# One TensorE signal per slot in the two gather stages of a two-layer GNN kernel

## The chip, the cores and the metric

The kernel runs on one core of a Trainium2 chip. The metric is the device time of one execution in microseconds (us). A core has five engines, each with its own instruction stream: TensorE (PE in the views, PEld for its weight loads), VectorE (DVE), ScalarE (ACT), GpSimd (POOL) and SyncE (SP, which here only issues DMAs). They meet through semaphores: an instruction or a DMA raises one when it is done, and another engine's stream waits until it has reached a number.

## The reference

Two message passing layers over the same 400,000 edges (sorted by destination) and 12,500 nodes, 64 features, all in float32:

```python
def gnn_layer_0(x, edge_attr, ...):
    msg = mlp(concat([x[row], edge_attr]))          # matmul, batch norm over all edges, SiLU
    agg = segment_sum(msg, col) / max(count(col), 1)
    return mlp(concat([x, agg]))

def gnn_layer_1(x, edge_attr, ...):
    msg = relu(x[src] + edge_attr)
    agg = segment_sum(msg, dst)
    return relu(((1 + eps) * x + agg) @ W.T + b)

x = layernorm(x + gnn_layer_0(x, edge_attr, ...))
x = layernorm(x + gnn_layer_1(x, edge_attr, ...))
```

## The kernel before, in words

The edges are worked off in G = 625 **slots** of EG = 640 edges, TG = 5 tiles of P = 128. There are four large steps, one after the other: **stage A** (L250 to L570) gathers x[src] for every edge, applies the first linear layer and stores the result; pass B (L598 to L720) normalises it, applies SiLU and sums it by segment; a node part (L900 to L1150) makes the new x and writes it to DRAM; **stage C** (L1150 to L1255) gathers the new x for every edge, adds, applies ReLU and sums by segment. A short output part ends the program. The change touches stages A and C alone.

**Stage A, one slot s.** SP loads the slot's edge features into half of the ring buffer `Z` (L357; RING = 10 slots). POOL gathers the 640 rows of x into the other half by five indirect DMAs (L371). PE transposes the five tiles of `Z` into PSUM (`turn_rows`, L399 to L407). ACT copies these five tiles to `ZT` in SBUF (L456; two buffers). PE applies W1 to `ZT` and, by five more small matmuls, counts the edges per destination (`dense`, L409 to L424). DVE takes statistics of two slots at a time, adds the counts into a table and copies the result to `h_ring` (`pair`, L518 to L531), and ACT issues the store of it (L449). DVE also builds the one-hot matrix `hot` that the counts are made with (`one_hot`, L504).

**Stage C, one slot s.** SP loads edge features into `E` (L1174), POOL gathers rows of the new x into `X` by five indirect DMAs (L1194), both rings of 10 slots. PE adds the two in PSUM by two matmuls with the identity (`edge_sum`, L1200 to L1209), ACT applies ReLU (L1235), PE sums by segment with five matmuls (`segment_sum`, L1211 to L1218), DVE adds the result into the table (`add`, L1249) and builds the one-hot matrices (L1244).

**What sets the order.** Every engine's order is written out by hand. On PE it is, in both stages, one step ahead: `turn_rows(s+1)`, `dense(s)`, `turn_rows(s+2)`, `dense(s+1)` and so on (`edge_sum` and `segment_sum` in stage C):

```python
for s in range(slots):
    if not (slots < BODY and s == slots - 1):
        turn_rows(k, s + 1)
    dense(k, s, slots < BODY and s == slots - 1)
```

PE raises **two semaphores per slot**. In stage A `rows_done` rises at the end of `turn_rows` and `dense_done` at the end of `dense`; in stage C `sum_put` rises at the end of `edge_sum` and `summed` at the end of `segment_sum`. Who waits for them:

- SP (L356, L1173) and POOL (L366, L1187) wait for `rows_done` or `sum_put` of the slot ten before, since that frees a place in the ring. POOL's wait is followed by a count of its own (`carry_wait`, L131).
- ACT, before it copies slot s, waits for `rows_done` of slot s and `dense_done` of slot s-2, which frees a buffer of `ZT` (L454, L455). In stage C it waits for `sum_put` of slot s and `summed` of slot s-5.
- DVE waits for `dense_done` (L505, L520) and `summed` (L1243, L1248).
- PE itself waits for the gathered rows, the edge features, ACT's and DVE's signals.

Of the kernel before, what the change touches and what calls it, by code (L numbers as in the profile page):

```python
# [55 lines left out]
def gnn_kernel(nc, x, src, dst, edge, W1, b1, g1, be1, W2, b2, g2, be2, W3, b3, eps1, out):  # L56
# [50 lines left out]
    with ctx:  # L107
# [118 lines left out]
        with ExitStack() as here:  # L226
# [109 lines left out]
            gathered = gathered_x  # L336
            rows_done = sem("rows_done")
            zt_taken = sem("zt_taken")
            dense_done = sem("dense_done")
            h_ready = sem("h_ready")  # L340
# [10 lines left out]
            with nc.Block() as block:  # L351
                @block.sync
                def _(sp):
                    def body(k, slots):
                        for s in range(slots):
                            wait_at(sp, rows_done, k, BODY, s + 1 - RING)  # L356
                            sp.dma_start(Z[:, s % RING, :, D:2 * D], edge_v[at(k, BODY, s)]).then_inc(e_loaded[s % RING], 16)  # L357

                    all_bodies(sp, body)
                    sp.wait_ge(s_x, 16)  # L360

                @block.gpsimd
                def _(pool):
                    for g in range(G):
                        r = g % RING
                        if g >= RING:  # L366
                            pool.wait_ge(rows_done, g + 1 - RING)
                            carry_wait(pool)
# [8 lines left out]
                def _(pe):  # L377
# [21 lines left out]
                    def turn_rows(k, s):  # L399
# [4 lines left out]
                        for j in range(TG):  # L404
                            last = nc.tensor.transpose(banks(2 * (s % 2), 2, P, EG)[:, j * P:(j + 1) * P],  # L405
                                                       Z[:, r, j, :], ident[:, :])
                        last.then_inc(rows_done, 1)  # L407

                    def dense(k, s, alone):  # L409
# [12 lines left out]
                        for j in range(TG):  # L422
                            last = nc.tensor.matmul(PS[0:D, bank + ab, HC:HC + WIN], ones_bf[:, :],  # L423
                                                    hot[:, q % 5, ab, j, :], start=(j == 0), stop=(j == TG - 1))  # L424
                        last.then_inc(dense_done, 1)

# [5 lines left out]

                    turn_rows(0, 0)
                    all_bodies(pe, body)
# [11 lines left out]
                def _(act):  # L446
# [5 lines left out]
                    def body(k, slots):  # L452
                        for s in range(slots):
                            act.wait_ge(rows_done, at(k, BODY, s + 1))  # L454
                            wait_at(act, dense_done, k, BODY, s - 1)  # L455
                            act.activation(ZT[:, s % 2, :], banks(2 * (s % 2), 2, P, EG), ACT.Copy).then_inc(zt_taken, 1)  # L456
                            if s % 2 == 1 and not (isinstance(k, int) and k == 0 and s == 1):
                                store(k, s // 2 - 1)
# [11 lines left out]
                def _(dve):  # L470
# [35 lines left out]
                    def one_hot(k, s):  # L506
                        wait_at(dve, dense_done, k, BODY, s + 1 - 10)
                        nc.vector.tensor_tensor(
# [9 lines left out]
                    def pair(k, q, firsts):  # L518
                        bank = 4 + 2 * (q % 2)
                        dve.wait_ge(dense_done, at(k, BODY, 2 * q + 2))  # L520
                        for c in range(2):
# [9 lines left out]
                    def body(k, slots):  # L531
# [8 lines left out]
                        if slots < BODY:  # L540
                            q = slots // 2
                            bank = 4 + 2 * (q % 2)
                            dve.wait_ge(dense_done, G)
                            nc.vector.bn_stats(stats[:, 6 * (G - 1):6 * G], PS[:, bank, 0:HC]).then_inc(stats_done, 1)
# [609 lines left out]
        with ExitStack() as here:  # L1154
# [6 lines left out]
            gathered = gathered_x1  # L1161
            sum_put = sem("sum_put")
            hot_ready = sem("c_hot_ready")
            msg_ready = sem("c_msg_ready")
            summed = sem("c_summed")
            added = sem("c_added")
            x1_kept = sem("x1_kept")

            with nc.Block() as block:
                @block.sync  # L1170
                def _(sp):
                    def load(k, s):
                        wait_at(sp, sum_put, k, BODY, s + 1 - RING)  # L1173
                        sp.dma_start(E[:, s % RING, :, :], edge_v[at(k, BODY, s)]).then_inc(e_loaded[s % RING], 16)  # L1174
# [11 lines left out]
                def _(pool):  # L1186
                    for g in range(G):  # L1187
                        r = g % RING
                        if g >= RING:
                            pool.wait_ge(sum_put, g + 1 - RING)  # L1190
                            carry_wait(pool)
# [8 lines left out]
                def _(pe):  # L1200
                    def edge_sum(k, s):
# [5 lines left out]
                        pe.wait_ge(gathered[r], at(k, 32 * TG, 16 * TG * (s // RING) + 16 * TG))  # L1207
                        nc.tensor.matmul(PS[:, s % 2, 0:HC], ident[:, :], X[:, r, :, :].rearrange("p t c -> p (t c)"),  # L1208
                                         start=False, stop=True).then_inc(sum_put, 1)  # L1209

                    def segment_sum(k, s):  # L1211
# [3 lines left out]
                        for j in range(TG):  # L1215
                            last = nc.tensor.matmul(PS[D:P, 2 + s % S, 0:WIN], msg[:, s % S, j, :], hot[:, s % S, j, :],  # L1216
                                                    start=(j == 0), stop=(j == TG - 1))
                        last.then_inc(summed, 1)  # L1218

# [5 lines left out]

                    edge_sum(0, 0)
                    all_bodies(pe, body)

                @block.scalar
                def _(act):  # L1230
                    def body(k, slots):
                        for s in range(slots):
                            act.wait_ge(sum_put, at(k, BODY, s + 1))
                            wait_at(act, summed, k, BODY, s + 1 - S)
                            act.activation(msg[:, s % S, :, :].rearrange("p t c -> p (t c)"), PS[:, s % 2, 0:HC],  # L1235
                                           ACT.Relu).then_inc(msg_ready, 1)
# [4 lines left out]
                def _(dve):  # L1241
                    def one_hot(k, s):
                        wait_at(dve, summed, k, BODY, s + 1 - S)  # L1243
                        nc.vector.tensor_tensor(  # L1244
# [4 lines left out]
                    def add(k, s, first):  # L1249
                        dve.wait_ge(summed, at(k, BODY, s + 1))  # L1250
                        wait_at(dve, added, k, BODY, s)
# [205 lines left out]
```

## Time and profile before

| what | value |
|---|---|
| time, median of 3 runs | 10121.98 us (10119.3 to 10125.19) |
| span of the profiled execution | 10108.7 us, 90454 instructions |
| what lies around the span, as against the median | 13.3 us |
| POOL busy | 5970.4 us (59%) |
| PE busy | 4398.6 us (44%) |
| DVE busy | 1864.3 us (18%) |
| ACT busy | 1239.0 us (12%) |
| DMA | 638.49 MB, mean 63 GB/s |

The profile is one execution recorded by the hardware profiler. Its page gives busy time by engine and the costliest groups of instructions; a further view lists who waited for whom, another lists instructions in order of time. The program has one core, so no other core's work stands in the trace. The profiled execution's own time is its span of 10108.7 us plus what lies around it (start and end of the program); the median of the runs is 13.3 us above the span. Releasers are inferred from semaphore events. Where the page cannot place the semaphore it says "remote", or it names a DMA that had used the same semaphore number earlier in the program. A semaphore's true source is read in the code.

### The profile page before, as it was taken

Reading aid. Unit: us, or ns where it says so; the run is one execution under the profiler, and the core shown is the slowest. Engines: PE = TensorE matmul, PEld = TensorE weight load, DVE = VectorE, ACT = ScalarE, POOL = GpSimd, SP = SyncE. Lnnn points to the kernel's source line nnn. Section 1 sums busy time; section 2 is a strip of 40 time slices with the busy share of each in tenths; the row PEclk is TensorE's granted clock in tenths of the full one; section 3 lists DMA queues with packets and bytes.
Section 4 is the critical chain, followed back from the end, with each engine's and each line's share of the span. In section 5 each row is a group of like instructions: output and inputs, shape, how many; then the busy total and the mean of one; then the engine's idle time right before and its main releaser. Section 6 shows DMA issues by size and latency. Waiting matters only on the chain. (4 is left out here: it accounts for less than half of the span.)

```text
span 10108.7 us, 90454 instructions
## 1 busy us (share of the span) xinstructions
PE 4398.6 (44%) x25778; PEld 2780.5 (28%) x25778; DVE 1864.3 (18%) x4868; ACT 1239.0 (12%) x2056; POOL 5970.4 (59%) x6272
## 2 busy tenths in 40 slices
PE   3433443434444444347984333333333334333335
PEld 1222222222222222226872222222222222222222
DVE  2111111111111111116763000000000000000002
ACT  0000000000000000004664000000000000000001
POOL 6666666666666666660003666666666666666662
PEclk7666666666666666668996666666666666666666
DMA  3222222222222222224551121121112212111111
GB/s 79 68 67 66 69 67 66 69 67 67 68 67 68 68 67 67 68 67 132 164 151 50 44 47 45 45 45 45 45 45 45 45 45 46 44 45 45 45 45 33
DMA packets 800217, 638.49 MB, mean 63 GB/s; under 512 B 532451, under 2 KB 618703, under 8 KB 799368
## 3 DMA queue, kind: packets, MB, share of 16 engines
q1 hardware_dynamic: 553308, 326.50, 12.0%
q0 software_dynamic: 200416, 208.55, 10.7%
q10 hardware_dynamic: 46400, 102.52, 3.1%
q14 instruction: 75, 0.61, 0.0%
q8 instruction: 18, 0.29, 0.0%
HBM read 528.15 MB, written 108.90 MB: 63 GB/s over the span
## 5 line engine op out<-in xcount | busy, mean ns | idle before, releaser
L1194 POOL DMA_INDIRECT X<-x_scratch,src_idx x3125 | 2971.8, 951 | 1624.3 <-issue 893.6
L371 POOL DMA_INDIRECT Z<-in_x_dram,src_idx x3125 | 2968.4, 950 | 1611.1 <-issue 895.1
L416 PE MATMUL PS<-ZT,W_sb 128*64 128x320 f32 x2500 | 1198.0, 620 | 2716.5 <-ACT ZT L456 2391.7
L1216 PE MATMUL PS<-hot_c,msg_c 128*64 128x48 f32 x6250 | 658.9, 271 | 2765.6 <-issue 1733.5
L1216 PEld LDWEIGHTS PS<-hot_c,msg_c 128*64 128x64 f32 x6250 | 575.0, 184 | 3163.0 <-issue 2048.4
L416 PEld LDWEIGHTS PS<-ZT,W_sb 128*64 128x64 f32 x2500 | 396.7, 185 | 3153.5 <-issue 2160.2
L522 DVE BATCH_NORM_STATS2 stats<-PS 128x320 f32 (+1 forms) x624 | 279.3, 490 | 3670.2 <-remote 3451.3
L456 ACT ACTIVATE ZT<-PS 128x640 f32<-128x640 f32 x625 | 425.2, 702 | 4150.2 <-remote 3395.5
L1252 DVE TENSOR_TENSOR table<-table,PS 64x48 f32 x625 | 130.2, 208 | 4057.3 <-DMA shares_scratch<-counts 3495.7
L1235 ACT ACTIVATE msg_c<-PS 128x320 f32<-128x320 f32 x625 | 260.0, 436 | 4295.3 <-DMA counts_scratch<-table 2919.9
L1205 PE MATMUL PS<-E,ident 128*128 128x320 f32 x1250 | 689.6, 644 | 11.8 <-DMA E<-in_edge_attr_dram 11.8
L405 PE MATMUL PS<-ident,Z 128*128 128x128 f32 x3125 | 635.1, 350 | 6.9 <-issue 6.9
L1208 PE MATMUL PS<-X,ident 128*128 128x320 f32 x1250 | 586.9, 560 | 24.4 <-DMA X<-x_scratch,src_idx 18.6
L405 PEld LDWEIGHTS PS<-ident,Z 128*128 128x128 f32 x3125 | 447.6, 178 | 254.5 <-issue 226.3
L650 PE MATMUL PS<-hot,msg 128*64 128x48 f32 x6250 | 427.2, 224 | 0.0
L650 PEld LDWEIGHTS PS<-hot,msg 128*64 128x64 f32 x6250 | 388.3, 138 | 52.6 <-issue 36.6
L977 POOL DMA_DIRECT2D counts_scratch<-table x1 | 0.6, 583 | 675.4 <-POOLq L123 675.4
L1208 PEld LDWEIGHTS PS<-X,ident 128*128 128x128 f32 x1250 | 320.5, 257 | 192.8 <-issue 118.8
L616 ACT ACTIVATE mT<-hT,shift_col,scale_col 128x640 f32<-128x640 f32 x313 | 285.2, 911 | 3.7 <-DMA hT<-h_scratch 3.7
L1244 DVE TENSOR_TENSOR hot_c<-window,rel 128x240 f32<-128x240 f32 x625 | 256.1, 410 | 114.9 <-issue 89.6
L527 DVE TENSOR_SCALAR h_ring<-PS,b1c 128x640 f32<-128x640 f32 x312 | 271.8, 871 | 0.0
L423 PEld LDWEIGHTS PS<-hot_a,ones_bf 128*64 128x64 bf16 x3125 | 226.5, 139 | 151.6 <-issue 128.1
(135 smaller groups left out, 2519.8 us busy)
## 6 DMA issues: line engine op xcount, KB each, us to landing
Z<-in_edge_attr_dram SPq DMA_DIRECT2D x625, 160.0 KB
E<-in_edge_attr_dram SPq DMA_DIRECT2D x625, 160.0 KB
h_scratch<-h_ring ACTq DMA_DIRECT2D x312, 320.0 KB
hT<-h_scratch SPq DMA_DIRECT2D x312, 320.0 KB
Z<-in_x_dram,src_idx POOLq DMA_INDIRECT x3125
X<-x_scratch,src_idx POOLq DMA_INDIRECT x3125
x_nodes<-in_x_dram SPq DMA_DIRECT2D x1, 3125.0 KB
x_ring<-in_x_dram SPq DMA_DIRECT2D x25, 125.0 KB
```

Of the source, the lines that this page charges most:

```text
L371: nc.gpsimd.indirect_dma_start(out=Z[:, r, j, 0:D], out_offset=None, in_=x, in_offset=bass.IndirectOffsetOnAxis(ap=src_idx[:, n:n + 1], ax ...
L405: last = nc.tensor.transpose(banks(2 * (s % 2), 2, P, EG)[:, j * P:(j + 1) * P], Z[:, r, j, :], ident[:, :])
L416: nc.tensor.matmul(PS[ab * D:(ab + 1) * D, bank + c, 0:HC], W1_sb[:, :], ZT[:, s % 2, c * HC:(c + 1) * HC], start=True, stop=True)
L456: act.activation(ZT[:, s % 2, :], banks(2 * (s % 2), 2, P, EG), ACT.Copy).then_inc(zt_taken, 1)
L522: nc.vector.bn_stats(stats[:, ds(at(k, 120, 12 * q + 6 * c), 6)], PS[:, bank + c, 0:HC]).then_inc(stats_done, 1)
L527: nc.vector.tensor_scalar(h_ring[:, q % 5, :].rearrange("p (c e) -> p c e", c=2), PS[:, bank:bank + 2, 0:HC], b1c[:, :], None, ALU.add).th ...
L616: act.activation(mT[0:parts, q % 5, :], hT[0:parts, q % 5, :], ACT.Silu, bias=shift_col[0:parts, :], scale=scale_col[0:parts, :]).then_inc ...
L650: last = nc.tensor.matmul(PS[D:P, 4 + 2 * (q % 2) + ab, 0:WIN], msg[:, q % 5, j, ab, :], hot[:, q % 5, ab, j, :], start=(j == 0), stop=(j ...
L1194: nc.gpsimd.indirect_dma_start(out=X[:, r, j, :], out_offset=None, in_=x1_dram, in_offset=bass.IndirectOffsetOnAxis(ap=src_idx[:, n:n + 1] ...
L1205: nc.tensor.matmul(PS[:, s % 2, 0:HC], ident[:, :], E[:, r, :, :].rearrange("p t c -> p (t c)"), start=True, stop=False)
L1208: nc.tensor.matmul(PS[:, s % 2, 0:HC], ident[:, :], X[:, r, :, :].rearrange("p t c -> p (t c)"), start=False, stop=True).then_inc(sum_put, 1)
L1216: last = nc.tensor.matmul(PS[D:P, 2 + s % S, 0:WIN], msg[:, s % S, j, :], hot[:, s % S, j, :], start=(j == 0), stop=(j == TG - 1))
```

## The change

In both stages PE raises one semaphore per slot, `pe_step`, in place of two. It rises once after the first slot's transposes (`turn_rows(0, 0)`, or `edge_sum(0, 0)`), and then at the end of each `dense(s)` or `segment_sum(s)`. So the value s + 1 now says that `dense(s-1)` is done, and, since PE works in the order above, that `turn_rows(s)` is done too. All waits are moved to it. POOL and SP now wait for the `dense` that follows the transposes of the slot ten before. ACT waits for `dense(s-1)` before it copies slot s, where it waited for `turn_rows(s)` and `dense(s-2)`. No matmul, copy or DMA is added, removed or moved in any engine's order; wait instructions and the register arithmetic for their numbers change.

```diff
@@ stage A @@
-            rows_done = sem("rows_done")
+            pe_step = sem("a_pe_step")
             zt_taken = sem("zt_taken")
-            dense_done = sem("dense_done")
...
-                            wait_at(sp, rows_done, k, BODY, s + 1 - RING)
+                            wait_at(sp, pe_step, k, BODY, s + 1 - RING)
...
-                            pool.wait_ge(rows_done, g + 1 - RING)
+                            pool.wait_ge(pe_step, g + 1 - RING)
...
                             last = nc.tensor.transpose(banks(2 * (s % 2), 2, P, EG)[:, j * P:(j + 1) * P],
                                                        Z[:, r, j, :], ident[:, :])
-                        last.then_inc(rows_done, 1)
+                        return last
...
                             last = nc.tensor.matmul(PS[0:D, bank + ab, HC:HC + WIN], ones_bf[:, :],
                                                     hot[:, q % 5, ab, j, :], start=(j == 0), stop=(j == TG - 1))
-                        last.then_inc(dense_done, 1)
+                        last.then_inc(pe_step, 1)
...
-                    turn_rows(0, 0)
+                    turn_rows(0, 0).then_inc(pe_step, 1)
...
-                            act.wait_ge(rows_done, at(k, BODY, s + 1))
-                            wait_at(act, dense_done, k, BODY, s - 1)
+                            act.wait_ge(pe_step, at(k, BODY, s + 1))
...
-                        wait_at(dve, dense_done, k, BODY, s + 1 - 10)
+                        wait_at(dve, pe_step, k, BODY, s + 2 - 10)
...
-                        dve.wait_ge(dense_done, at(k, BODY, 2 * q + 2))
+                        dve.wait_ge(pe_step, at(k, BODY, 2 * q + 3))
...
-                            dve.wait_ge(dense_done, G)
+                            dve.wait_ge(pe_step, G + 1)
@@ stage C @@
-            sum_put = sem("sum_put")
+            pe_step = sem("c_pe_step")
...
-            summed = sem("c_summed")
...
-                        wait_at(sp, sum_put, k, BODY, s + 1 - RING)
+                        wait_at(sp, pe_step, k, BODY, s + 1 - RING)
...
-                            pool.wait_ge(sum_put, g + 1 - RING)
+                            pool.wait_ge(pe_step, g + 1 - RING)
...
-                        nc.tensor.matmul(PS[:, s % 2, 0:HC], ident[:, :], X[:, r, :, :].rearrange("p t c -> p (t c)"),
-                                         start=False, stop=True).then_inc(sum_put, 1)
+                        return nc.tensor.matmul(PS[:, s % 2, 0:HC], ident[:, :],
+                                                X[:, r, :, :].rearrange("p t c -> p (t c)"), start=False, stop=True)
...
-                        last.then_inc(summed, 1)
+                        last.then_inc(pe_step, 1)
...
-                    edge_sum(0, 0)
+                    edge_sum(0, 0).then_inc(pe_step, 1)
...
-                            act.wait_ge(sum_put, at(k, BODY, s + 1))
-                            wait_at(act, summed, k, BODY, s + 1 - S)
+                            act.wait_ge(pe_step, at(k, BODY, s + 1))
...
-                        wait_at(dve, summed, k, BODY, s + 1 - S)
+                        wait_at(dve, pe_step, k, BODY, s + 2 - S)
...
-                        dve.wait_ge(summed, at(k, BODY, s + 1))
+                        dve.wait_ge(pe_step, at(k, BODY, s + 2))
```

## Rows read from the trace of the kernel before

**Rows 1.** The page: span and busy time of each engine.
```profile
span 10108.7 us, 90454 instructions
PE 4398.6 (44%) x25778; PEld 2780.5 (28%) x25778; DVE 1864.3 (18%) x4868; ACT 1239.0 (12%) x2056; POOL 5970.4 (59%) x6272
```

**Rows 2.** The page's groups: line, engine, operation, count | busy, mean ns | idle before, releaser.
```profile
L1194 POOL DMA_INDIRECT X<-x_scratch,src_idx x3125 | 2971.8, 951 | 1624.3 <-issue 893.6
L371 POOL DMA_INDIRECT Z<-in_x_dram,src_idx x3125 | 2968.4, 950 | 1611.1 <-issue 895.1
```

**Rows 3.** The waits: engine, line <- releaser: us in total, times, longest us.
```profile
POOL Z L371 <- issue: 895.1, 2938, 0.3
POOL Z L371 <- remote: 694.6, 180, 9.9
POOL X L1194 <- DMA counts_scratch<-table: 643.7, 168, 11.6
...
ACT msg L622 <- PE PS L644: 216.9, 312, 1.3
```

**Rows 4.** Timeline of POOL: start us, us, line, operation [idle before <-releaser].
```profile
2004.07 0.94 POOL L371 DMA_INDIRECT Z<-in_x_dram,src_idx  x1 [0.30 <-issue]
2009.63 1.11 POOL L371 DMA_INDIRECT Z<-in_x_dram,src_idx  x1 [4.62 <-remote]
...
2033.59 0.98 POOL L371 DMA_INDIRECT Z<-in_x_dram,src_idx  x1 [0.30 <-issue]
2039.01 0.95 POOL L371 DMA_INDIRECT Z<-in_x_dram,src_idx  x1 [4.44 <-remote]
```

**Rows 5.** Timeline of PE and ACT about the first of these two stops.
```profile
1987.84 0.77 PE L405 MATMUL PS<-ident,Z 128*128 128x128 f32 x5
1995.33 2.39 PE L416 MATMUL PS<-ZT,W_sb 128*64 128x320 f32 x4 [6.72 <-issue]
1997.91 1.33 PE L405 MATMUL PS<-ident,Z 128*128 128x128 f32 x5
...
1994.50 0.70 ACT L456 ACTIVATE ZT<-PS 128x640 f32<-128x640 f32 x1 [10.02 <-remote]
2008.86 0.70 ACT L456 ACTIVATE ZT<-PS 128x640 f32<-128x640 f32 x1 [13.65 <-remote]
```

**Rows 6.** Timeline of pass B, where POOL has no work: PE, then ACT.
```profile
4701.31 0.77 PE L644 MATMUL PS<-ident,mT 128*128 128x128 f32 x5
4702.19 0.49 ACT L622 ACTIVATE msg<-PS 128x384 f32<-128x384 f32 x1 [0.69 <-PE PS L644]
```

**Rows 7.** Timeline of ACT between the two stops, and of PE behind one copy.
```profile
2010.29 0.70 ACT L456 ACTIVATE ZT<-PS 128x640 f32<-128x640 f32 x1 [0.74 <-DVE h_ring L527]
2013.14 0.70 ACT L456 ACTIVATE ZT<-PS 128x640 f32<-128x640 f32 x1 [2.14 <-issue]
2019.87 0.70 ACT L456 ACTIVATE ZT<-PS 128x640 f32<-128x640 f32 x1 [6.03 <-remote]
2038.24 0.70 ACT L456 ACTIVATE ZT<-PS 128x640 f32<-128x640 f32 x1 [17.66 <-remote]
...
92.05 0.70 ACT L456 ACTIVATE ZT<-PS 128x640 f32<-128x640 f32 x1 [29.50 <-remote]
...
94.99 0.46 PE L423 MATMUL PS<-hot_a,ones_bf 128*64 128x48 bf16 x5
```

**Rows 8.** Timeline of the start of stage C: ACT, DVE, PE.
```profile
5471.37 0.44 ACT L1235 ACTIVATE msg_c<-PS 128x320 f32<-128x320 f32 x1 [10.28 <-PE PS L1208]
5487.27 0.44 ACT L1235 ACTIVATE msg_c<-PS 128x320 f32<-128x320 f32 x1 [15.47 <-DMA counts_scratch<-table]
5526.47 0.44 ACT L1235 ACTIVATE msg_c<-PS 128x320 f32<-128x320 f32 x1 [38.76 <-DMA counts_scratch<-table]
...
5476.83 0.21 DVE L1252 TENSOR_TENSOR table<-table,PS 64x48 f32 x1 [30.58 <-DMA shares_scratch<-counts]
5515.39 0.21 DVE L1252 TENSOR_TENSOR table<-table,PS 64x48 f32 x1 [37.91 <-DMA shares_scratch<-counts]
...
5469.90 1.43 PE L1208 MATMUL PS<-X,ident 128*128 128x320 f32 x2 [8.21 <-DMA X<-x_scratch,src_idx]
5471.26 1.30 PE L1216 MATMUL PS<-hot_c,msg_c 128*64 128x48 f32 x10
5479.73 1.43 PE L1208 MATMUL PS<-X,ident 128*128 128x320 f32 x2 [5.80 <-issue]
```

## The prediction, on record before the changed kernel was run

> **What bounds the kernel now.** I read the page first. POOL is busy 59% of the span, more than any other engine, and PE 44% [rows 1]. The page's two largest groups are POOL's gathers of stages A and C, 3,125 each, with 2968.4 + 1611.1 us and 2971.8 + 1624.3 us of busy and idle time [rows 2]. So stage A takes 4579.5 us of POOL's stream and stage C 4596.1 us, together 9175.6 of 10108.7 us. All else (pass B, nodes, output) is 933 us and not touched.
>
> Then the waits tell of what the idle time is made. A gather costs 0.95 us plus 0.30 us of issue (895.1 us in 2938 times), so 1.25 us, and a slot of five 6.25 us. This part is POOL's own. The other part is waits for a place in the ring, which PE's signal frees: 694.6 us in 180 times in stage A, 643.7 us in 168 times in stage C [rows 3]. (The releaser is called "remote" and "DMA counts_scratch"; by the code it is `rows_done` and `sum_put`.)
>
> The timeline of POOL shows their rhythm: a stop of 4.62 us, 20 gathers without a pause, a stop of 4.44 us [rows 4]. From 2009.63 to 2039.01 are 29.38 us for four slots, or 7.35 us a slot; 4579.5 / 625 is 7.33. So the kernel is bound by POOL, plus one stop of some 4.4 us every four slots.
>
> Why does POOL stop? Not because PE is slow: it is idle more than half the time. PE's **signals come late**. At 1994.50 ACT copies a slot, PE works on the copy at 1995.33 and transposes the slot after the next at 1997.91. The transposes of the next slot had therefore been those that ended at 1987.84 + 0.77 = 1988.61. ACT's copy of that slot starts at 2008.86, 20.2 us later, after 13.65 us of idle time [rows 5]. Its second condition, the `dense` before the last, was older still. In pass B, where POOL does nothing, the transposes end at 4702.08 and ACT starts at 4702.19, 0.11 us later, and no such wait exceeded 1.3 us in 312 [rows 3, 6]. So while POOL gathers, a signal of PE can take ten to twenty us, and when POOL has stopped the pending ones arrive together.
>
> The lateness grows with the number of signals in line. At the start of stage C both signals can be read from their readers. The first `edge_sum` in these rows ends at 5471.33 and ACT starts at 5471.37. The `segment_sum` behind it ends at 5472.56; DVE starts at 5476.83, 4.3 us late. The next `edge_sum` ends at 5481.16; ACT starts at 5487.27, 6.1 us late. Then signals wait behind each other, and the readers start at 5515.39 and 5526.47 [rows 8]: 28 and 11 us between deliveries, and (5526.47 - 5471.37) / 4 = 13.8 us a signal over the four. In the steady cycle it is mixed: ACT's four copies start at 2010.29, 2013.14, 2019.87 and 2038.24 [rows 7]. The first few signals after a stop pass quickly, later ones only one in 14 us or so, or with the next stop.
>
> **The change, part by part.** It takes away 625 signals in each stage, 1,250 in all, adds none, and moves no instruction. ACT has one wait less a slot, which is under its 13 to 30 us idle stretches [rows 5, 7] and costs or gives nothing. Three effects are left.
>
> *Fewer signals in line.* A cycle of four slots needs eight signals now. By my reading three to four come with the stop (the rows of ACT at 2008.86 and 2010.29 are of such a group) and four to five while POOL works 25 us. With one signal a slot, the same four to five deliveries beside POOL's work free four to five slots, not two.
>
> *A chain of signals.* ACT's copy of slot s now waits for `dense(s-1)`, and `dense(s)` waits for that copy. So at most one signal is pending at a stop, and the stop frees one slot, not two. A slot costs at least the way from ACT's start to the end of `dense`: 95.45 - 92.05 = 3.40 us [rows 7]. That lies under POOL's 6.25 us. In stage C the same way is 0.44 us and 1.30 us of matmul [rows 8], shorter.
>
> *A later release of the ring place*, by one `dense` (about 3 us of those 3.40). POOL stands there only when it is at a stop, and there the chain above counts it already: nothing more.
>
> The sum: a cycle after the change has 1 slot from the stop and 4 to 5 from deliveries beside POOL, so N = 5 to 6. With the same stop of 4.4 us, a slot costs (6.25 N + 4.4) / N = 7.13 us for 5 and 6.98 us for 6. I take the middle, 7.05, against 7.35: 0.30 x 1,250 = 375 us less. 10108.7 - 375 = 9733.7 of span, plus the 13.3 us around it by which the median of the runs exceeds it: **9747 us**. The bounds of the unknown price, N = 4 and N = 8 (the nearest rows give 4 now, and 8 is one stop in a ring's length), give 7.35 and 6.80 us: 10122 and 9434 us.
>
> What a signal costs PE itself is not on the path, since PE idles. The trace shows delays of 4 to 20 us, and pending signals arriving within one stop [rows 5, 8]. The Trainium skill (TensorE: Matmul & The Clock Gate, Part 3, "The cost: per-tile semaphore tail") fits about 26 ns for every increment on a matmul; by it 1,250 fewer would be 33 us of an engine with slack, and the sum would be no change. The measured delays speak against that being the whole price here.
>
> **The rivals.**
>
> *The stops vanish (chance 0.23).* If signals 6.25 us apart always pass as the one at 5471.33 did (nothing had been signalled for 10 us), POOL never waits. Then the two sums of waits go, less the 0.30 us of issue that each of the 348 would still have: 694.6 + 643.7 - 104.4 = 1234 us, so 8888 us. For it: the quick deliveries after a pause. Against it: the 6.1 us delay of the signal at 5481.16 came with none in line before it, 4.3 us after the last delivery, and 3.40 + 6.1 is more than 6.25.
>
> *The chain is too slow (0.15), slower than before.* If what holds signals back is how long POOL has been working and not how many were sent, then the first 8 us after a stop let pass what PE can make in that time, and that is now a chain of 3.40 us and more a slot: two slots; with the one that the stop frees, three. Then N = 3 and a slot costs (18.75 + 4.4) / 3 = 7.72 us: +0.37 x 1,250 = +460, or 10584 us. It decides where the third link's signal is held until the stop. For it: before the change PE had up to four signals in line to make use of a stop, now one. Against it: 2019.87 is 10 us after POOL's restart and a signal still came through [rows 4, 7].
>
> *The count does not matter (0.12).* Both effects cancel or signals are cheap, as the skill's rule has it. What the stop frees falls from two slots to one, what passes beside POOL rises from two to three, N stays 4: 10122 us.
>
> *The forecast (0.50)*: its own range is 9434 to 10122 us.
>
> **How the numbers follow.** 0.2% of the time, 20 us, is about what can be told from no change. The forecast gives 0.46 faster and 0.02 each to same and slower; the vanished stops 0.23 faster; the slow chain 0.15 slower; the cancelling 0.03 faster, 0.06 same, 0.03 slower. Sum: faster 0.72, same 0.08, slower 0.20. The range starts at 8850, just below the case without stops, and ends at 10400, which leaves out the slow chain's full price and holds the rest.
>
> **What would show it.** In the profile after: the stops of POOL fewer than 348 (about 230 for N = 5.5), each still near 4.4 us; runs of 25 to 30 gathers between them; POOL's busy time and 0.30 us of issue unchanged; ACT's copies still late by many us, but for `dense`. The rival without stops would show POOL's waits for the ring near zero. The slow chain would show runs of 15 gathers. I am wrong in kind if the runs of gathers stay 20 long, or if POOL's stops grow in length rather than number.

## The result, and the profile after

| | before | changed | ratio |
|---|---|---|---|
| time, median (4 runs each, same chip) | 10121.97 us | 10178.03 us (10173.78 to 10183.75) | 1.0054 [1.0043, 1.0066] |
| span of the profiled execution | 10108.7 us | 10175.0 us | |

The change makes the kernel slower by 0.5%. The forecast was 375 us faster. The page and the two largest groups of its section 5, as in [rows 1, 2]:

```profile
span 10175.0 us, 90051 instructions
PE 4538.9 (45%) x25778; PEld 2854.5 (28%) x25778; DVE 1865.3 (18%) x4868; ACT 1270.3 (12%) x2056; POOL 5995.9 (59%) x6272
...
L1191 POOL DMA_INDIRECT X<-x_scratch,src_idx x3125 | 2973.6, 952 | 1657.4 <-issue 904.7
L370 POOL DMA_INDIRECT Z<-in_x_dram,src_idx x3125 | 2992.0, 957 | 1616.0 <-issue 848.8
```

POOL's stream (busy and idle) grew in stage A from 4579.5 to 4608.0 us and in stage C from 4596.1 to 4631.0 us. These 63.4 us are nearly all of the span's 66.3. The time is lost where it was to be won, in POOL's gathers. The waits of the changed kernel (columns as in [rows 3]):

```profile
POOL Z L370 <- issue: 848.8, 2749, 4.3
POOL Z L370 <- remote: 746.8, 372, 5.9
...
POOL X L1191 <- DMA counts_scratch<-table: 676.6, 167, 10.8
```

The waits for the ring were to go from 348 to about 230. They went up to 539. In stage A they doubled in number and halved in mean length, with 746.8 in place of 694.6 us. But this view also counts gaps of 0.3 us, which is POOL's own issue, where a signal came in just then. Stops of over 1 us are the better count: behind the first 101 gathers, 208 in place of 156 in stage A and 156 in place of 139 in stage C. Now the timeline of POOL in the changed kernel, at the place of [rows 4]:

```profile
2019.77 0.94 POOL L370 DMA_INDIRECT Z<-in_x_dram,src_idx  x1 [4.26 <-remote]
...
2039.11 0.95 POOL L370 DMA_INDIRECT Z<-in_x_dram,src_idx  x1 [0.68 <-issue]
...
2049.12 0.95 POOL L370 DMA_INDIRECT Z<-in_x_dram,src_idx  x1 [4.07 <-remote]
```

From stop to stop are 29.35 us and 20 gathers; before it was 29.38 us and 20 gathers [rows 4]. Half the signals, and here the rhythm is the same. Over the whole stage it is not: before the change 145 of the 155 intervals from stop to stop are of 20 gathers, after it 78 of 207 are of 20, 78 of 15 and 47 of 5. Stage C never had the rhythm of [rows 4], which is of stage A. There the usual run was 25 gathers before the change (97 of 138 intervals) and is 20 after it (148 of 155), as two stops of each show, before and then after:

```profile
8052.23 0.95 POOL L1194 DMA_INDIRECT X<-x_scratch,src_idx  x1 [5.06 <-DMA counts_scratch<-table]
...
8088.45 0.95 POOL L1194 DMA_INDIRECT X<-x_scratch,src_idx  x1 [5.20 <-DMA counts_scratch<-table]
```
```profile
8016.60 0.95 POOL L1191 DMA_INDIRECT X<-x_scratch,src_idx  x1 [4.40 <-DMA counts_scratch<-table]
...
8045.78 0.95 POOL L1191 DMA_INDIRECT X<-x_scratch,src_idx  x1 [4.42 <-DMA counts_scratch<-table]
```

25 gathers in 36.22 us became 20 in 29.18 us: the runs became shorter in both stages, and the pace hardly changed. Last, ACT and PE in the same stretch:

```profile
2018.99 0.70 ACT L454 ACTIVATE ZT<-PS 128x640 f32<-128x640 f32 x1 [9.94 <-remote]
2022.22 0.70 ACT L454 ACTIVATE ZT<-PS 128x640 f32<-128x640 f32 x1 [2.52 <-remote]
2026.97 0.70 ACT L454 ACTIVATE ZT<-PS 128x640 f32<-128x640 f32 x1 [4.04 <-PE PS L422]
2038.33 0.70 ACT L454 ACTIVATE ZT<-PS 128x640 f32<-128x640 f32 x1 [10.66 <-remote]
2048.35 0.70 ACT L454 ACTIVATE ZT<-PS 128x640 f32<-128x640 f32 x1 [9.31 <-remote]
```
```profile
2019.76 0.46 PE L422 MATMUL PS<-hot_a,ones_bf 128*64 128x48 bf16 x5
2027.74 0.34 PE L422 MATMUL PS<-hot_a,ones_bf 128*64 128x48 bf16 x5
```

PE's `dense` ends at 2019.76 + 0.46 = 2020.22 and at 2028.08. ACT's next copies, which wait for just these signals, start at 2022.22 and at 2038.33. By the chain only one signal is ever on its way, and it still needs 2.0 and 10.3 us. So these two are not late because they stand in line behind another.

### The profile page after: what moved, and what is told of

It reads as the page before. It is cut to its first block and busy times, and to the rows that moved or that the text cites. A ratio compares the mean times of both kernels' runs of the same rounds, so it can differ in the third digit from the quotient of the medians.

```text
span 10175.0 us, 90051 instructions
## 1 busy us (share of the span) xinstructions
PE 4538.9 (45%) x25778; PEld 2854.5 (28%) x25778; DVE 1865.3 (18%) x4868; ACT 1270.3 (12%) x2056; POOL 5995.9 (59%) x6272
## 5 line engine op out<-in xcount | busy, mean ns | idle before, releaser
L415 PE MATMUL PS<-ZT,W_sb 128*64 128x320 f32 x2500 | 1224.9, 632 | 2705.7 <-ACT ZT L454 1614.6
L1213 PE MATMUL PS<-hot_c,msg_c 128*64 128x48 f32 x6250 | 688.7, 278 | 2705.5 <-issue 2334.0
L1213 PEld LDWEIGHTS PS<-hot_c,msg_c 128*64 128x64 f32 x6250 | 604.7, 192 | 3123.6 <-issue 2733.2
L1202 PE MATMUL PS<-E,ident 128*128 128x320 f32 x1250 | 724.5, 674 | 11.8 <-DMA E<-in_edge_attr_dram 11.8
L1205 PE MATMUL PS<-X,ident 128*128 128x320 f32 x1250 | 617.6, 587 | 24.6 <-DMA X<-x_scratch,src_idx 17.9
L1202 PEld LDWEIGHTS PS<-E,ident 128*128 128x128 f32 x1250 | 261.5, 261 | 60.3 <-DMA E<-in_edge_attr_dram 12.2
```

The costliest lines, as they stand in the source:

```text
L415: nc.tensor.matmul(PS[ab * D:(ab + 1) * D, bank + c, 0:HC], W1_sb[:, :], ZT[:, s % 2, c * HC:(c + 1) * HC], start=True, stop=True)
L1202: nc.tensor.matmul(PS[:, s % 2, 0:HC], ident[:, :], E[:, r, :, :].rearrange("p t c -> p (t c)"), start=True, stop=False)
L1205: return nc.tensor.matmul(PS[:, s % 2, 0:HC], ident[:, :], X[:, r, :, :].rearrange("p t c -> p (t c)"), start=False, stop=True)
```

## The experiments

All results first. Ratios are against the kernel before on the same chip (its median was 10061.6 to 10062.7 us beside e1 to e6, e10 and e11, and 10119.5 us beside the others, so times of different rows don't compare). Where no ratio stands, one run was made, and the kernel's result is not the reference's, since it leaves out gathered rows.

| run | what it is | time, us | ratio |
|---|---|---|---|
| e1 | the change in stage A alone | 10080.72 | 1.0017 [1.0008, 1.0026] |
| e2 | the change in stage C alone | 10070.92 | 1.0008 [0.9999, 1.0017] |
| e3 | four signals per slot | 10064.14 | 1.0003 [0.9993, 1.0012] |
| e4 | one signal per slot, given early | 10051.94 | 0.9992 [0.9983, 1.0001] |
| e5 | stage C on plain loads, no gather | 6801.45 | |
| e6 | e5, POOL busy with memsets | 7148.75 | |
| e7 | stage C: the sum on VectorE | 10134.59 | 1.0012 [1.0002, 1.0022] |
| e8 | stage A: two slots per round trip | 10110.34 | 0.9991 [0.9981, 1.0000] |
| e9 | e7 and e8 | 10124.47 | 1.0005 [0.9995, 1.0015] |
| e10 | the change again, another chip | 10090.08 | 1.0030 [1.0019, 1.0042] |
| e11 | the chain alone, two signals | 10095.86 | 1.0037 [1.0023, 1.0050] |
| e12 | stage C: gathers that nobody waits for | 10969.02 | |
| e13 | a pause of 0.22 us behind each gather | 10790.18 | 1.0660 [1.0629, 1.0691] |
| e14 | a pause of 0.11 us | 10117.15 | 0.9995 [0.9984, 1.0007] |
| e15 | stage C: each gather half as many rows | 10130.15 | |

### The number of signals, and the chain

**e1** and **e2** are the parts of the change's diff under "stage A" and "stage C", each alone.

> Stage A has one signal per slot, stage C keeps two. The profile of the changed kernel gives stage A 28.5 us more of POOL's stream (4608.0 against 4579.5) and stage C 34.9 us more (4631.0 against 4596.1). If the loss arises in both, each from its own stage: about +29 us, 10151. Rival: only the total counts (what one stage loses shifts the other): anything else, such as no loss here and all of it in stage C.

> Stage C has one signal per slot, stage A keeps two. By its own stage: about +35 us, 10157. Rival as for the run with stage A alone.

Stage A costs 0.17%, some 19 us where 29 were expected; stage C costs 0.08%, some 9 us where 35 were expected, and that can't be told from nothing. The two profiles, taken on one chip, each hold one stage with the change and one without it: POOL's stream is 4563.5 us in stage A with it and 4549.4 without, in stage C 4586.3 and 4572.3. That is 14 us for each stage. Neither part alone carries the loss.

**e10** is the changed kernel again, on the same chip as e11 below (10061.74 us before):

> The changed kernel again, beside the kernel before on the same chip. Its first comparison gave +0.54%; the two stages alone gave +0.17% and +0.08% on another chip. If the parts add, +0.25% here; if the first comparison holds for every chip, +0.5%.

It loses 0.30% there, and 0.54% in the first pair. The sign holds. 0.30% is close to the sum of the parts; why the first pair shows nearly twice as much is open.

**e3** doubles the count: a semaphore that nobody reads, raised in the middle of each of PE's four blocks.

```diff
+            unread = sem("a_unread")
...
+                            if j == 1:
+                                last.then_inc(unread, 1)
                         last.then_inc(rows_done, 1)
```

> The kernel before with two more signals per slot from TensorE in both stages, on matmuls in the middle of each group, to a semaphore that nobody waits for: four signals a slot. Theory of the prediction (the number of signals in line makes them late, 14 us or so for each under POOL's work): 1250 more per stage would more than double the stops, 11000 us or more. New theory (a signal is late by where it falls in POOL's run of gathers, not by how many there are): within 0.5% of 10122.

Nothing: 1.0003. If signals waited for each other as the prediction had it, four a slot had to cost several per cent. The Trainium skill (TensorE: Matmul & The Clock Gate, Part 3, "The cost: per-tile semaphore tail") has about 26 ns for one increment, from which 2,500 more would be, as an estimate, 65 us of an engine that idles half the time. This run shows that the number costs the kernel nothing here; what one increment costs TensorE it does not show.

**e4** keeps one signal per slot, and gives it at the end of the transposes, so that ACT's copy needs nothing of the slot before: no chain.

```diff
-                        last.then_inc(rows_done, 1)
+                        last.then_inc(pe_step, 1)
...
-                        last.then_inc(dense_done, 1)
+                        if slots < BODY and s >= slots - 2:
+                            last.then_inc(pe_step, 1)
...
-                            wait_at(act, dense_done, k, BODY, s - 1)
...
-                        dve.wait_ge(dense_done, at(k, BODY, 2 * q + 2))
+                        dve.wait_ge(pe_step, at(k, BODY, 2 * q + 4))
```

> One signal per slot as in the change, but given at the end of the transposes (stage A) or of the edge sum (stage C) of the slot that TensorE does ahead, so ScalarE's copy of slot s does not wait for the matmuls of slot s-1: as few signals as in the change, without its chain; VectorE learns of a finished slot two transposes later. If the chain ate the gain of fewer signals: faster than 10122 by the forecast's 1 to 4%. If the number does not matter: within 1% of 10122, either side.

Halving the signals without the chain loses nothing, and gains at most 0.17%.

**e11** is the other half: two signals as before, but the chain.

```diff
-                            wait_at(act, dense_done, k, BODY, s - 1)
+                            wait_at(act, dense_done, k, BODY, s)
...
-                            wait_at(act, summed, k, BODY, s + 1 - S)
+                            wait_at(act, summed, k, BODY, s)
```

> The kernel before with its two signals per slot; only ScalarE's wait is tightened, so that the copy of slot s waits for the matmuls of slot s-1 in both stages, as the change has it. If the chain is what makes the change slower: the same loss as the change in this call. If the later freeing of the ring is what does it (POOL and SyncE wait for the matmuls behind the transposes, here they do not): no loss here.

It loses 0.37% [0.23, 0.50], as much as the whole change in e10. With e4 this settles the loss on this chip: it is ACT's wait for the matmuls of the slot before, not the signal that was removed, and not the later release of the ring, which e11 does not have. What then bounds POOL was open.

### What makes the signals late

**e5** takes POOL's gathers out of stage C; SP loads 640 fixed rows in their place.

```diff
+                        sp.dma_start(X[:, s % RING, :, :], rows).then_inc(gathered[s % RING], 16)
...
-                            nc.gpsimd.indirect_dma_start(
```

> Stage C takes 640 fixed rows per slot by a plain load that SyncE issues, POOL has no work there (the gather is left out, so the output is not the reference's). If POOL's gathers hold TensorE's signals back: they arrive within 0.1 us, as in pass B, no wait of ScalarE's or VectorE's of over 5 us, and stage C takes what TensorE or the loads need, 2.5 to 4 us a slot, 1600 to 2500 us instead of 4600. Rival (the pattern of TensorE's own short work and idle gaps in this stage makes signals late): still waits of 10 us and more.

**e6** adds 1500 memsets on POOL beside it:

```diff
+                    for _ in range(1500):
+                        chain.link(nc.gpsimd.memset(idle[:, :], 0.0))
```

> As the run with plain loads, but POOL clears a buffer nobody reads 1500 times during stage C (about 1 us each). If it is POOL being busy that holds signals back: waits of 10 us and more come back for the first 1500 us of the stage. If it is the gathers themselves (their descriptors or their DMA): signals stay within 0.1 us.

One row each of a stretch of stage C, e5 and then e6 (us; busy us and instructions of PE, PEld, DVE, ACT, POOL; granted clock, DMA share, GB/s):

```profile
5450.00:6700.00 1250.00, 1236.52 (x8637) 825.56 (x8638) 379.14 (x1230) 272.36 (x621) 0.00 (x0) 0.99 0.54 162
```
```profile
5450.00:6700.00 1250.00, 1224.15 (x8620) 822.67 (x8620) 379.33 (x1230) 269.48 (x615) 1183.16 (x1166) 0.99 0.54 162
```

Both work some 620 slots in these 1250 us, 2.0 us a slot and not 7.3 (2.5 to 4 were expected), with a DMA share of 0.54; POOL at 1183 us of memsets takes nothing from it. In both runs every one of ACT's 625 copies starts within 0.12 us of TensorE's latest `edge_sum`; in the kernel before 416 of 625 start more than 1 us behind it. e6's longer time is only POOL finishing its memsets, which end at 7030 us. So a busy POOL does not hold signals back, nor does a higher rate of plain transfers. Its gathers do.

**e12** is the counterpart: the computation on plain loads as in e5, and POOL gathers as ever, into a ring that nobody reads. It waits for its own landings alone.

```diff
-                            pool.wait_ge(sum_put, g + 1 - RING)
+                            pool.wait_ge(gathered[r], 16 * TG * (g // RING))
...
-                                out=X[:, r, j, :], out_offset=None, in_=x1_dram,
+                                out=apart[:, r, j, :], out_offset=None, in_=x1_dram,
```

> Stage C: POOL does all 3125 gathers into a ring that nothing reads, waiting only for the landing of its own gathers of ten slots before; the other engines compute on plain loads as in the run with plain loads (the gathered rows are left out of the result). Theory A (TensorE is what is held back; POOL can run at its own 1.25 us a gather): POOL's gathers take 3906 us without stops, and TensorE's steps are slowed for as long as they run. Theory B (the gathers themselves are served at 7.3 us a slot, and POOL has to stop in the end wherever it waits): POOL's stretch is about 4550 us even with nobody to wait for. The time per slot of the other engines beside it says how far the gathers alone slow TensorE: 2.0 us a slot without gathers.

Two stretches of it, while POOL gathers and after it has ended (columns as above), then PE and ACT in the first:

```profile
5600.00:9600.00 4000.00, 377.65 (x1428) 236.56 (x1428) 62.90 (x204) 44.62 (x102) 3035.56 (x2862) 0.51 0.15 32
9850.00:10850.00 1000.00, 998.35 (x7049) 671.19 (x7048) 310.02 (x1006) 220.01 (x503) 0.00 (x0) 1.00 0.54 162
```
```profile
8038.19 1.27 PE L1213 MATMUL PS<-X,ident 128*128 128x320 f32 x2
8075.01 1.27 PE L1221 MATMUL PS<-hot_c,msg_c 128*64 128x48 f32 x10 [35.55 <-issue]
...
8035.22 0.44 ACT L1240 ACTIVATE msg_c<-PS 128x320 f32<-128x320 f32 x1 [38.82 <-remote]
8074.47 0.44 ACT L1240 ACTIVATE msg_c<-PS 128x320 f32<-128x320 f32 x1 [38.82 <-issue]
```

With POOL gathering without a stop, ACT does 102 slots in 4000 us, one in 39 us; without POOL 503 in 1000 us. The chain is plain to read: PE's last matmul ends at 8039.46, ACT starts 35.0 us later. ACT's own signal passes at once: it ends at 8074.91 and PE starts at 8075.01. Only TensorE's side is held back. And the second finding: POOL, which now waits for nobody, needs 6.98 us a slot over its gathers 101 to 3001, not 6.25, and not the 7.3 of the rival theory: the result lies between the two that were expected. The group of its gathers, and two rows of its timeline:

```profile
L1199 POOL DMA_INDIRECT apart<-x_scratch,src_idx x3125 | 3302.9, 1057 | 1122.4 <-issue 1049.0 <-POOLq L123 73.5
...
5682.84 1.13 POOL L1199 DMA_INDIRECT apart<-x_scratch,src_idx  x1 [0.30 <-issue]
5684.27 1.79 POOL L1199 DMA_INDIRECT apart<-x_scratch,src_idx  x1 [0.30 <-issue]
```

A gather takes 1057 ns on average where it took 951 [rows 2]. The first 180 gathers of the stage go out 1.26 us apart; from 5684.27 on some 200 of the 2,943 that are left take 1.7 to 1.95 us in place of 0.95, with the usual 0.30 us before them. So 1.25 us is a pace that POOL can't keep: left alone it gets to 6.98 / 5 = 1.40 us.

### Other structures that should shorten the stops

**e7** moves stage C's first sum to VectorE, four slots ahead, so that the ring does not wait for TensorE, and ACT waits for it only with `segment_sum` of five slots before:

```diff
-                            pool.wait_ge(sum_put, g + 1 - RING)
+                            pool.wait_ge(msg_ready, g + 1 - RING)
...
+                        nc.vector.tensor_tensor(E[:, r, :, :], E[:, r, :, :], X[:, r, :, :],
+                                                ALU.add).then_inc(sum_put, 1)
```

> Stage C of the kernel before with the sum of edge features and gathered rows on VectorE, four slots ahead, and the ring freed by ScalarE, so no step on POOL's or ScalarE's way waits for a fresh signal of TensorE; TensorE's own signals may be four slots late. Theory (a signal of TensorE is 10 us late or more under the gathers, and what costs is each round trip TensorE to ScalarE to TensorE): POOL's stops in stage C go from about 650 us to under 150, 500 to 600 us less, 9500. Rival (the gathers hold back VectorE's signals too, or POOL must stop for its own sake about 4 us in 29): stops stay, within 1% of before.

POOL's timeline in e7, a stop and the next, then PE before and at the end of such a stop:

```profile
7922.04 0.94 POOL L1195 DMA_INDIRECT X<-x_scratch,src_idx  x1 [10.67 <-ACT msg_c L1223]
...
7995.97 0.95 POOL L1195 DMA_INDIRECT X<-x_scratch,src_idx  x1 [10.98 <-ACT msg_c L1223]
```
```profile
8042.11 0.24 PE L1207 MATMUL PS<-hot_c,msg_c 128*64 128x48 f32 x1 [2.55 <-issue]
8044.90 0.24 PE L1207 MATMUL PS<-hot_c,msg_c 128*64 128x48 f32 x1 [2.56 <-issue]
8047.70 0.24 PE L1207 MATMUL PS<-hot_c,msg_c 128*64 128x48 f32 x1 [2.56 <-issue]
...
8073.60 1.31 PE L1207 MATMUL PS<-hot_c,msg_c 128*64 128x48 f32 x11 [1.16 <-issue]
```

The stop mostly comes once in nine or ten slots, and is 11 us long here: 73.9 us for 50 gathers, 7.39 us a slot (7.30 over the stage). And not signals alone are late: single matmuls start 2.8 us apart while POOL gathers, and of ten such rows, which make a block of `segment_sum`, only the first has a wait ahead of it. When POOL has stood since 8066.8, eleven run in 1.3 us. VectorE's signals stay in time: in all 625 slots ACT starts within 0.12 us of the end of VectorE's sum. The gain of 500 to 600 us that was expected did not come.

**e8** makes the round trip in stage A for two slots at a time (ZT four deep, one `rows_done`, one copy, one `dense_done` a pair), and **e9** is both.

```diff
-                            pool.wait_ge(rows_done, g + 1 - RING)
+                            pool.wait_ge(rows_done, g // 2 - 4)
...
-                        last.then_inc(dense_done, 1)
+                        if ab == 1 or alone:
+                            last.then_inc(dense_done, 1)
```

> Stage A of the kernel before with two slots to each round trip: ten transposes, one signal, one copy by ScalarE, then the matmuls of both. If each round trip costs one late signal whatever it carries: about eight slots between POOL's stops in place of four, 4.4 us / 8 in place of 4.4 / 4 per slot, some 340 us less in stage A, 9720. Rival (POOL stops for its own sake): no change.

> Both of these edits together. They lie in stages apart, so the two gains add: about 9200 if the theory holds in both.

Both are within 0.2% of no change, where gains of at least 340 and of some 900 us were expected. All these profiles say the same when POOL's stops are counted (idle time over 1 us ahead of a gather, behind the first 101 gathers of the stage):

| kernel, stage | stops | mean, us | sum, us | us a slot |
|---|---|---|---|---|
| before, A | 156 | 4.32 | 674 | 7.30 |
| before, C | 139 | 4.45 | 618 | 7.25 |
| changed, A | 208 | 3.30 | 687 | 7.35 |
| changed, C | 156 | 4.27 | 665 | 7.30 |
| e3, C | 121 | 5.04 | 610 | 7.22 |
| e7, C | 71 | 8.73 | 620 | 7.30 |
| e8, A | 140 | 4.49 | 628 | 7.30 |

The number of stops varies by a factor of three, their sum by 13%. Who waits for whom decides how the pause is cut up, hardly how long it is. (13% is 77 us, more than the loss of the change: this table shows why nothing was to be won, not where the 0.3 to 0.5% went.)

The kernel before shows the same without any experiment, once its stops are sorted by the gathers since the last one, and e8 and e11 bear it out:

| kernel, stage | gathers since the last stop | stops | mean, us |
|---|---|---|---|
| before, A | 20 | 145 | 4.40 |
| before, C | 25 | 97 | 5.06 |
| e8, A | 10, 20, 30 | 23, 72, 44 | 3.29, 4.14, 5.66 |
| e11, A | 15, 20, 25 | 55, 72, 14 | 3.27, 3.82, 4.53 |

From row to row a stop grows by 0.09 to 0.15 us with each gather before it. Added to the 1.25 us of a gather this gives, as an estimate, 1.34 to 1.40 us, and e12 has 1.40.

### Pace and size of the gathers

**e13** and **e14** put a small memset behind each gather, and POOL waits for it; 128x128 elements in e13, 128x1 in e14.

```diff
                             ).then_inc(gathered[r], 16)
+                            chain.link(nc.gpsimd.memset(idle[:, :], 0.0))
```

> The kernel before with a small clear on POOL (128 columns, about 0.2 us, and a wait for it) behind every gather in both stages: a gather every 1.5 us or so. Theory A1 (something behind the gathers is served at about 1.46 us a gather, piles up while POOL is faster, and TensorE is held back until the pile is gone): no stops, TensorE's signals in time, 7.5 to 7.8 us a slot, 10250 to 10650. Theory A2 (TensorE is held back whenever POOL gathers, however slowly): the stops stay and add, 8.5 us a slot or more, 11500 or more.

> As the other paced run with the shortest clear (one column, about 0.1 us): a gather every 1.35 to 1.45 us. A1: POOL's stops shrink by what its gathers grow, so the sum stays 7.3 to 7.4 us a slot, 10060 to 10180. A2: the stops stay, 7.35 us and the clears on top, 10500 or more.

The timeline of stage C in e14: POOL's first gather of two slots, and a slot of PE, ACT and DVE between:

```profile
8001.66 0.94 POOL L1201 DMA_INDIRECT X<-x_scratch,src_idx  x1 [0.83 <-issue]
8002.60 0.11 POOL L1205 MEMSET idle_c<- 128x1 f32 x1
...
8008.86 0.94 POOL L1201 DMA_INDIRECT X<-x_scratch,src_idx  x1 [0.83 <-issue]
```
```profile
8002.15 1.44 PE L1216 MATMUL PS<-X,ident 128*128 128x320 f32 x2 [3.30 <-DMA X<-x_scratch,src_idx]
8003.63 0.44 ACT L1243 ACTIVATE msg_c<-PS 128x320 f32<-128x320 f32 x1 [6.77 <-PE PS L1216]
```

At 1.33 us a gather and 7.20 us a slot (7.28 over the stage) the stops of 4 us are gone, and PE's matmul (end 8003.59) is followed by ACT after 0.04 us; PE now waits for the gathered rows. In stage C 27 of 625 copies of ACT still start more than 1 us behind TensorE's latest `edge_sum`, in place of 416; in stage A, against the latest transposes, it is some 260 in place of some 460, so part of the lateness stays there. The time stays: 0.9995, as expected. POOL pauses 0.08 us more behind each gather and 0.56 us more at each slot (0.83 for 0.27 us), 0.95 us a slot over its 6.25, in place of the 618 us of stops in 580 slots of stage C, which are 1.07 us a slot. In e13 a slot is 7.84 us by POOL's own pace, and the kernel 6.6% slower, above the 10250 to 10650 us that were expected: from here on a pause is a loss.

**e15** gathers 64 of the 128 rows in stage C.

```diff
-                                out=X[:, r, j, :], out_offset=None, in_=x1_dram,
+                                out=X[0:D, r, j, :], out_offset=None, in_=x1_dram,
```

> The kernel before, but each gather of stage C fetches 64 rows in place of 128 (the other half of the partitions stays zero, so half of the gathered rows are left out of the result). If what piles up behind POOL is served by the row or byte (7.3 us a slot for 640 rows, 3.65 for 320), it never piles up: TensorE's signals come within 0.1 us, POOL does not stop but for its own pace (6.25 us a slot or less), stage C takes 3906 us or less, 9370 or less in all. If it is served by the gather whatever its size: no change, 10120.

The group and timeline of its gathers:

```profile
L1197 POOL DMA_INDIRECT X<-x_scratch,src_idx x3125 | 2798.4, 896 | 1737.8 <-issue 888.5 <-DMA counts_scratch<-table 838.1 <-PE PS L1211 11.0
...
8016.13 0.89 POOL L1197 DMA_INDIRECT X<-x_scratch,src_idx  x1 [5.39 <-DMA counts_scratch<-table]
...
8045.24 0.89 POOL L1197 DMA_INDIRECT X<-x_scratch,src_idx  x1 [5.42 <-DMA counts_scratch<-table]
```

Half the rows and bytes, and 20 gathers still take 29.11 us. POOL issues them faster (1.20 us) and stands longer: 811 us of stops in the stage in place of 618. So between 64 and 128 rows the limit is per gather, not per row or byte.

## Why the prediction was wrong

**Right: what bounds the kernel.** POOL's gathers plus its stops do. The lateness of PE's signals while POOL gathers was read rightly too, and e5 and e12 show it: 2.0 us a slot without gathers, 39 with gathers that never pause.

**Wrong: "The lateness grows with the number of signals in line".** This is the step that failed, and with it the term "fewer signals in line" (375 us). It was read from four deliveries at the start of stage C [rows 8], where more signals in line and a longer time of POOL's gathering come together. The runs part them: four signals a slot cost nothing (e3), one a slot without a chain gains nothing that can be told (e4), and in the changed kernel a lone signal is 10.3 us late. The N = 5 to 6 that followed did not come; the stops came after 15 and 20 gathers in stage A and after 20 in stage C.

**Wrong: the stop as a fixed price of 4.4 us** that is paid less often if more slots pass between. The stop grows with the gathers before it: 4.4 us after 20, 5.1 after 25, 9.8 on average after 50 (e7), or 0.95 us in each slot (e14). The sum hardly changes with how it is cut up. So (6.25 N + 4.4) / N was the wrong form whatever N is. Stage C had N = 5 already before the change, which the prediction, with rows of stage A alone, took for 4; by its formula that is 7.13 us a slot, and the stage took 7.25. The lower ends of the range, 6.80 us at N = 8 and 6.25 us without stops, were not to be had in stage C: POOL alone does 6.98 there (e12). The forecast's 7.05 is not excluded by that, but no kernel here with stops went below 7.21.

**The chain: right in place, wrong in size.** The forecast let it free one slot less at a stop and added nothing else. The rival "the chain is too slow" had the mechanism and the sign, at +460 us, and its sign in the profile, runs of 15 gathers, is there in stage A. e11 has it at +0.37%, some 35 us. It was too large because it, too, took the stops as fixed. That the first pair shows 0.54% for all of the change is outside what e11 explains.

**"The count does not matter"** (10122 us) was the nearest case. Of its two readings, that signals are cheap held (e3); the other, that two effects cancel, did not, since there was nothing for the chain to cancel against.

**What would show it.** Runs of 25 to 30 gathers were to come, and "wrong in kind" was to be known by runs that stay 20 long. It is worse than that: stage A's went from 20 to 15 and 20, stage C's from 25 to 20.

**What stays open.** The runs fit one account: something behind POOL serves a gather in 1.40 to 1.46 us, POOL issues one in 1.25, and while unserved ones have piled up TensorE's own issue and signals wait, until POOL has stood long enough. What this something is, and why TensorE is late where ScalarE's and VectorE's signals are not, no run shows. Nor does a trace tell whether a matmul or its signal is late, since the ends of matmuls in it are modelled. Nor is it shown why POOL takes 7.2 to 7.35 us a slot with its stops and 6.98 without. A rival is that a stop lasts as long as TensorE needs for the work it could not do while POOL gathered. Against it: e7 takes TensorE's busy time in stage C from 1805 to 987 us, and the stops still sum to 620 us, for 618. Why the chain costs 0.3 to 0.4% was not parted further either; in the changed kernel's stage A, 23.6 us of the loss are gathers that take 957 in place of 950 ns, and e1 has the same (959 ns).

No kernel here beats the one before by more than can be told: e4 (0.9992) and e8 (0.9991) come nearest.

## What to carry to other kernels

When an engine stops for another one's late signal, first find out whether the stop is the cause or the remedy: make the waits rarer (e7) or the stream slower by a known pause (e14), and see whether the sum of idle time follows. Sorting the stops by the length of the run before them asks the same of a trace that is already there. If the sum doesn't follow, the stream's own rate is the likely limit. Fewer signals won't help then; fewer instructions of the stream might, which no run here tried. And one signal in place of two is free only if the one kept comes as early as the readers need it: merging into the later one adds a wait that the old pair did not have.

## What the runs showed of the hardware that was not expected

- Indirect DMAs from GpSimd are issued at 1.25 us each, but not sustained at that: 1.40 us when nobody else limits them (e12), 1.45 to 1.47 us with the stops of the kernels before, changed, e7 and e8, and 1.45 us with 64 rows as with 128 (7.27 and 7.25 us a slot in stage C, e15 and before).
- While such gathers go on unpaused, TensorE is held back and ScalarE and VectorE are not: signals of TensorE come 35 us late (e12), single matmuls 2.8 us apart (e7). ScalarE's signal in the same rows of e12 needs 0.1 us, VectorE's at most 0.12 us in e7. GpSimd's memsets at 95% busy don't do it (e6), nor plain transfers at 162 GB/s (e5).
- A memset of 0.11 us behind each gather (1.33 us from one to the next, 7.20 us a slot) ends nearly all of the lateness in stage C at no cost (e14); in stage A part of it stays.
- The granted clock follows: 0.51, a little above the lower of its levels (1.2 GHz), where TensorE works 378 of 4000 us, and 1.00, the upper (2.4 GHz), where it works 998 of 1000 (e12). In e14's stage C it was 0.54 in place of 0.64 and TensorE busy 2535 in place of 1805 us, and the time was the same, since TensorE was not the bound.
